# Recurrent state updates issued in four quarters instead of two halves on TensorE, with the output products of the same step dealt out between them

## The reference

```python
x = x + layernorm(attn(layernorm(x)))
x = x + layernorm(ffn(layernorm(x)))

# attn: rk = normalised heads of x, wk = rk shifted by one position, v = x @ Wv.T
def step(S, inp):                      # S: 32 x 32 for each sequence and head
    pred = einsum('bhk,bhkd->bhd', wk_t, S)
    err = (v_t - pred) * b_t[..., None]
    S = S + wk_t[..., None] * err[..., None, :]
    o = einsum('bhk,bhkd->bhd', rk_t, S) * g_t[..., None]
    return (S, o)
# then out @ Wo.T
```

## Time and profile before

| | |
|---|---|
| runs | 2305.5, 2309.14, 2312.44 us; median 2309.14 |
| profiled execution | 2322.8 us |
| its span, first to last instruction | 2321.1 us |
| busy: TensorE, VectorE, ScalarE, GpSimd | 90%, 86%, 77%, 75% |
| mean granted TensorE clock | 0.968 |

### The profile page before, as it was taken

How to read it: one execution, slowest core, us unless ns; L and a number is a source line. 1 busy time by engine, 2 the same in 40 slices (tenths; PEclk the granted TensorE clock), 3 DMA queues, 4 the chain that set the end, 5 groups by cost and what they waited for, 6 DMA issues and landing times. The chain is left out here.

```text
span 2321.1 us, 123730 instructions
## 1 busy us (share of the span) xinstructions
PE 2087.1 (90%) x50216; PEld 1317.7 (57%) x50216; DVE 1995.2 (86%) x5810; ACT 1776.4 (77%) x3756; POOL 1730.2 (75%) x3099
## 2 busy tenths in 40 slices
PE   1679999999999999999999999999999987499997
PEld 1346666666666666666656666666666654255554
DVE  5388999999999999999989899999999984588886
ACT  3767888888888888888888888888888744477775
POOL 2668888888888888888888888888888854143443
PEclk7789999999999999999999999999999988799999
DMA  2122333333333333333333333333333322488885
GB/s 87 50 61 77 99 96 98 101 97 96 100 97 96 96 94 96 94 94 96 94 92 94 94 97 94 94 96 98 95 93 96 82 77 67 149 221 228 225 232 129
DMA packets 156632, 247.69 MB, mean 107 GB/s; under 512 B 39544, under 2 KB 39552, under 8 KB 156064
## 3 DMA queue, kind: packets, MB, share of 16 engines
q1 hardware_dynamic: 156064, 239.78, 36.5%
HBM read 104.40 MB, written 67.11 MB: 74 GB/s over the span
## 5 line engine op out<-in xcount | busy, mean ns | idle before, releaser
L800 DVE TENSOR_TENSOR ps_elim<-ps_elim,sys 128x30 f32<-128x30 f32 (+14 forms) x1920 | 544.1, 327 | 0.7
L808 DVE TENSOR_TENSOR sys<-sys,ps_elim 128x30 f32<-128x30 f32 (+14 forms) x1920 | 535.8, 317 | 1.0
L925 PE MATMUL ps_v<-wv,xt 128*128 128x512 f16 x1536 | 436.6, 390 | 45.3 <-DVE rhs L831 20.4
L925 PE MATMUL ps_y<-wo,ot 128*128 128x512 f16 x1536 | 409.6, 387 | 23.4 <-DMA key_bd<-key_t 10.9
L962 PEld LDWEIGHTS ps_chain<-rhs,t_t 32*32 32x32 f32 x16384 | 257.3, 144 | 107.1 <-issue 107.0
L962 PE MATMUL ps_chain<-rhs,t_t 32*32 32x32 f32 x16384 | 285.9, 218 | 11.6 <-DVE rhs L831 5.9
L709 ACT ACTIVATE state<-ps_s 128x512 f32<-128x512 f32 x128 | 76.5, 598 | 258.8 <-PE ps_s L1024 258.7
L1024 PEld LDWEIGHTS ps_s<-err,key_b 32*32 32x32 f32 x16384 | 172.2, 106 | 139.5 <-issue 139.1
L1310 PE MATMUL ps_f<-wq,f_xq 128*128 128x512 f16 x1024 | 242.5, 381 | 6.8 <-DVE f_xq L1276 6.8
L925 PEld LDWEIGHTS ps_v<-wv,xt 128*128 128x128 f16 x1536 | 121.3, 99 | 195.4 <-issue 128.4
L1024 PE MATMUL ps_s<-err,key_b 32*32 32x32 f32 x16384 | 205.1, 195 | 27.0 <-issue 27.0
(11 more groups left out here) (163 smaller groups left out, 5116.6 us busy)
## 6 DMA issues: line engine op xcount, KB each, us to landing
x_in<-in_L_attn_x SPq DMA_DIRECT2D x128, 256.0 KB
kbd<-kt SPq DMA_DIRECT2D x512, 64.0 KB, 2.1
key_bd<-key_t SPq DMA_DIRECT2D x512, 64.0 KB
x_res<-in_L_attn_x SPq DMA_DIRECT2D x128, 256.0 KB
x_scratch<-x SPq DMA_DIRECT2D x128, 256.0 KB, 6.4
f_x<-x_scratch SPq DMA_DIRECT2D x32, 1024.0 KB, 7.8
out<-f_res SPq DMA_DIRECT2D x128, 256.0 KB, 3.9
gate<-gates SPq DMA_DIRECT2D x128, 7.9 KB
```

The lines of the kernel that those rows point to most:

```text
L800: dve.tensor_tensor(tmp, factors(r, c, first, end)[:, c - first:C - 1 - first, c - first:c - first + 1].to_broadcast(shape), sys[:, r, c:c ...
L808: dve.tensor_tensor(dst, dst, tmp, ALU.add).then_inc(elim_done[r], 1)
L925: last = pe.matmul(out, lhs[:, a, kb, :], weights[:, w, kb, :], start=(i == 0), stop=(i == 3 * KB - 1))
```

## The change

Inside one step of TensorE the update is issued in four quarters of 16 blocks (two trace records each) instead of two halves of 32. The output products stand as 1, 1 | 2 | 2 | 2 between the quarters and 4 behind, instead of 2, 1 | 3 between the halves and 6 behind. The two semaphore waits of `update_ready` (`keyb_done`, `err_done`) now stand before the second output product, not the third.

```diff
-            def blocks(half):
+            def blocks(part, parts=2):
-                for h in range(half * H // 2, (half + 1) * H // 2):
+                for h in range(part * H // parts, (part + 1) * H // parts):
                     for b in range(B):
...
-                def update(half):
+                def update(quarter):
                     if live:
-                        for h, q, e in blocks(half):
+                        for h, q, e in blocks(quarter, 4):
...
-                output(0, SHARE - 1)
+                output(0, 1)
                 update_ready(base, j)
-                output(SHARE - 1, SHARE)
+                output(1, 2)
                 update(0)
-                output(SHARE, 2 * SHARE)
-                last = update(1)
+                output(2, 4)
+                update(1)
+                output(4, 6)
+                update(2)
+                output(6, 8)
+                last = update(3)
                 if live:
                     last.then_inc(s["s_psum"], 1)
...
-                output(2 * SHARE, WHOLE - 1)
+                output(8, WHOLE - 1)
                 if y_live:
                     chain_ready(base, j + 1)
                 last = output(WHOLE - 1, WHOLE)
```

## The result

The changed kernel takes 2336.34 us (median of 4 runs, 2329.93 to 2340.85) where the one before takes 2310.79 beside it (4 runs, 2305.5 to 2313.52): a ratio of 1.010, 95% interval 1.0075 to 1.0124. It is slower. The profiled execution took 2329.93 us with a span of 2328.2 and a granted clock of 0.968. It lies at the lower end of its runs, while the profiled execution of before lies above all of its plain runs; so the two spans differ by 7.1 us and the medians by 25. I read the mechanism from the traces and the size from the ratios.

A forecast was written before the change was run, and what follows sets the result against it. Bound: a two-step loop through VectorE, TensorE, ScalarE's copies and `turn_back`. 0.43 + 0.44 = 0.87 us per critical step, less waits and pauses, gave +22 us on 2309.14: 2331 us, range 2303 to 2346.

The forecast's parts named there:

- `turn_back` is held by ScalarE's copy, so a later `state` is not won back: TensorE's `turn_back` waits for ScalarE's copy L611, so it comes the full 0.87 us later.
- The price on the way to `state`: Ahead of the update's end: two moved products +0.43 us, two extra array turns +0.44, so `s_psum` 0.87 us later.
- The rival in which turns are free in short bursts: Array turns around update blocks cost 0 instead of 0.44 us, leaving about +5 us; no chance of its own given.
- The earlier wait costs nothing: Waits on `err_done` and `keyb_done`, one output product earlier on TensorE, were priced at nothing.
- The pauses shrink by what is put ahead of them: TensorE's instruction-refill pauses in or behind the update get up to 0.87 us shorter with more work ahead.
- the rival that blamed the long bursts: Long update bursts starve TensorE and shorter ones end the pauses: about -10 us, 2299 us; chance 0.12.
- The sum: Costs over critical steps by stretch, less waits and pauses: +8.4, +5.4, +3, +2, +3, giving +21.8 us.
- A cost once a pair, with 1.5 us of room in the other step: Only the step whose `turn_back` VectorE waits for pays 0.87 us; the other hides delays under 1.5 us or so.
- a sign that the prediction had named: VectorE's wait at `rhs` grows from 1.2 to 2 us in critical steps.
- The prediction's third rival: Both steps of a pair become critical, through later ScalarE results such as `g_den`: 2353 us; chance 0.10.
- What swallows part of it: Waits for `x_res` behind `rhs` absorb delay: 2.0 us from 153 to 490 us, 10.1 us of waits from 1320 to 1850.
- The rival that had the waits swallow nearly all of it: Turns cheap, and `x_res` waits and pauses take up the rest: +3 us, 2312 us; chance 0.18.

The follow-up runs named there:

- e11: Changed kernel with ScalarE's `ps_zn` (L733) moved from behind the gates to ahead of the wait for the update's end; ratio to before 0.9977.
- e4: Changed kernel with ScalarE's copy L611 put ahead of the sum (L604); ratio to before 1.0103.
- e6: Changed kernel with L611 ahead of the sum and the copy `gram` (L674) ahead of `o_part`, `ss_ln` and `rn`; ratio to before 1.0099.
- e1: Update in four quarters, but six output products ahead of its last block and six behind, as in the kernel before; ratio to before 1.0024.
- e2: Kernel before, update still in two halves, but with eight output products ahead of the second half and four behind; ratio to before 1.0017.
- e3: Kernel before with only `update_ready` moved from ahead of the third output product to ahead of the second; ratio 1.000.
- e8: Kernel before with two output products moved the other way: four ahead of the update's second half and eight behind; ratio 1.0081.
- e7: Kernel before with 32 small transposes issued once ahead of the first step, no step changed; ratio 0.9976.
- e10: Kernel before with two implied TensorE waits dropped (768 instructions a step, not 770) and 60 small transposes ahead of the first step; ratio 1.0045.
- e5: The changed kernel timed once more, on the chip of the experiments; ratio to before 1.0076.
- e9: Kernel before with two implied TensorE waits dropped (768 instructions a step, not 770) and 12 small transposes ahead of the first step; ratio 0.9883.
- e12: Changed kernel with the edit of e9 (two waits dropped, 12 transposes ahead of the first step); ratio to before 0.9975.

## Why the prediction was right, and where it was not

The forecast was 2331 us, slower, and it came to 2336. Point by point:

- **`turn_back` is held by ScalarE's copy, so a later `state` is not won back.** Right: TensorE got the visible wait the prediction named (0.35 forecast, 0.39 measured), the row from `state` to the end of L611 stayed at 3.83 (374.17 to 378.00; 3.9 forecast), ScalarE's wait for `s_psum` grew from 1.60 to 2.5. e11 shows it by the other side. But "the copy L611" was too narrow: e4 and e6 took it out of the way and gained nothing, since the same row is met again at L674 and L681.
- **The price on the way to `state`.** Right, both terms: 0.42 for the turns against 0.44 (e1), 0.44 for the products against 0.43 (e2), 0.88 together against 0.87. The rival in which turns are free in short bursts is out. By the Trainium skill (TensorEngine Tiling (Array Packing), Key Properties), a change of tiling mode drains the engine. e1 agrees in that each turn costs time, and gives the price, about 0.2 us for a turn there and back.
- **The earlier wait costs nothing.** Right: e3, 1.000.
- **The pauses shrink by what is put ahead of them.** Right in the trace: 19.3 us in 25 steps became 1.1 in 4, e8 made them longer by the opposite edit, and e7 and e10 show that the place in the stream makes them, which takes out the rival that blamed the long bursts. (The prediction had none "in the other stretches"; the kernel before has 3.0 us in 4 steps from 153 to 490 us and 2.8 in 3 from 1320 to 1850.) A saving shows in the profiled executions: the 33 steps from 844 to 1329 us took 484.8 us before and 482.3 in the changed kernel (485.1 in e5), while the same steps took 470.7 in e9 and 477.2 in e12, 6.5 more. It does not show in the medians: with the pauses gone from both kernels the change costs 1.0093, with them in place 1.0076 to 1.010. The sum had eased its second and third stretch by 17 us (half of 11.8, and 11 of 13.9); the ratios leave room for some 9 us at most, by the intervals of both comparisons taken together. This term of the sum was too large.
- **A cost once a pair, with 1.5 us of room in the other step.** This is the step of the mechanism that failed. I had taken the loop over two steps, through VectorE, as the pace of the changed kernel too. The room at `rhs` was real, but `turn_back` also starts TensorE's own 6.59 us up to the next update, and that way has no room: TensorE and ScalarE alone form a loop of one step, 13.56 us before and 14.33 now. Before, two of them (27.1) were less than the pair's 28.0; now two of them (28.66) are more, and the quiet steps of the changed kernel and of e12 are 14.33. An undisturbed pair pays the difference, some 0.7 us, not 0.87, and it pays whether or not VectorE waits. With it fell a sign that the prediction had named: VectorE's wait at `rhs` was to grow from 1.2 to 2 us in critical steps, and its mean grew by 0.03 us from 850 to 1320 us (28.9 in 16 steps, now 29.4 in 16), by 0.11 from 490 to 850, and by about 0.3 in the two other stretches (18.6 to 22.6 in 12, 27.4 to 32.4 in 18). The prediction's third rival saw that both steps could turn critical, but through `g_den` and with the cost doubled; neither was so.
- **What swallows part of it.** `x_res` was to swallow 2.0 us at the start and most of 10.1 in the last stretch. Those waits are gone from the changed kernel's lists of these two stretches; in e5, the same kernel, 4.7 us of them stand from 1320 to 1850 us. How much of the loss they took was not tried by itself. The rival that had the waits swallow nearly all of it (+3 us) is out by both comparisons.
- **The size.** Of the 22 us of the sum, the medians gave 25.6, e5 17 to 18 and e12 against e9 21.4. That the sum fits is in part luck. 0.7 us a pair over 127 steps would be 44 us; less came because steps of before were longer than 14.0 us on the mean in most of the kernel (14.25 from 488 to 844 us, 14.69 to 1329, 14.41 to 1819, for pauses and transfers), and a changed kernel that takes 14.42, 14.61 and 14.36 there loses nothing it had already lost. The sum reached a like number with 0.87 in every pair and larger savings by pauses. By stretch, from the `state` starts of the profiled executions (one execution each; the two of the changed kernel differ by 10 us):

| steps | forecast, us | changed - before | e5 - before | e12 - e9 |
|---|---|---|---|---|
| first 24, to about 490 us | 8.4 | 5.3 | 4.9 | 2.1 |
| next 25, to 850 | 5.4 | 4.2 | 4.6 | 1.1 |
| next 33, to 1330 | 3 | -2.5 | 0.3 | 6.5 |
| next 33, to 1805 | 2 | -1.6 | 5.4 | 6.7 |
| last 12 | 3 | 5.7 | 6.0 | 5.3 |
| all | 21.8 | 11.0 | 21.3 | 21.7 |

The first stretch was forecast too dear and the last too cheap, and the total hides it.

## What to carry to other kernels

List the loops by their length before pricing an edit: a loop that is shorter than the bound today (here TensorE and ScalarE, 13.56 against 14.0 a step) costs little until an edit lengthens it past the bound, and then costs every step. When a wait is removed by moving one operation up, look whether the same producer is waited for again a little later: if its row of work is unbroken, as ScalarE's was here, the wait only moves (e4, e6), and what helped here is to move work into the producer's idle time (e11). Compare kernels whose instruction streams are of different length with care: a kernel of dense small products can differ by 1.6% through where its steps fall in the stream alone (e9 against e10).

## What the runs showed of the hardware

- 32 transposes ahead of the loop moved TensorE's pauses from 850 to 1320 us to 380 to 850 us (e7); a step of 768 instructions kept them at one place (32 of 32 steps in e10) or out of the update (e9). The Trainium skill, Runtime: NRT & Kernel Launch, Instruction fetch mechanics, says that crossing a 16 KiB block is mostly hidden. Here two packets of three land without a pause, and the third costs one when its place is in the dense small products: 0.78 us a pause on the mean in e10, 1.3 at most, and 1.6% of the kernel between the two places.
- A turn of the array to 32 x 32 blocks and back costs about 0.2 us (0.42 for two, e1), in bursts of 32 records as in those of 64.
- The edit of e9 gained 1.2% on the kernel before, and the same edit about 1.0% on the changed one (0.9975 against 1.0076), although the latter shows only 1.1 us of pauses inside the update from 850 to 1320 us. The edit also drops two waits; e10, which drops them too, shows that on the kernel before the place alone makes 1.6%. What the changed kernel gained it by is not settled.
